# A three-layer compressed interaction network in fp32: PE transposes moved to the end of a period, ReLU copies split in two, four places for high parts

## The reference

```python
LAYER_SIZE = [200, 200, 200]; SPLIT_HALF = True        # x: (512, 39, 32)
for i in range(3):
    z = jnp.einsum('bmd,bnd->bmnd', x, hidden).reshape(B, -1, D)
    cur = jnp.einsum('bcd,co->bod', z, Ws[i]) + bs[i][None, :, None]
    cur = jax.nn.relu(cur)
    if i != 2: hidden, direct = cur[:, :100, :], cur[:, 100:, :]
    else:      direct = cur
    finals.append(direct)
result = jnp.sum(jnp.concatenate(finals, axis=1), axis=-1)   # (512, 400)
```

## Time and profile before

| | |
|---|---|
| median of 3 runs | 3346.16 us (3346.16, 3346.29, 3316.85) |
| profiled execution, own time | 3314.96 us |
| its span, first to last instruction | 3313.2 us |
| PE, DVE, ACT busy | 2899.5, 2725.9, 1619.3 us |
| mean granted TensorE clock | 0.922 of full |

### The profile page before, as it was taken

The page is one execution under the profiler, slowest core; times in us unless marked ns, Lnnn a source line. Parts: engine busy times, 40 slices in busy tenths (PEclk is TensorE's granted clock), DMA queues, the critical chain, the costliest instruction groups (busy, mean ns, idle before and its releaser), DMA issues.

```text
span 3313.2 us, 51577 instructions
## 1 busy us (share of the span) xinstructions
PE 2899.5 (88%) x17960; PEld 2844.1 (86%) x17960; DVE 2725.9 (82%) x2725; ACT 1619.3 (49%) x2212; POOL 0.7 (0%) x7
## 2 busy tenths in 40 slices
PE   3788888888888889998998899989998999899988
PEld 3788888888888888888888888888888888888888
DVE  5788888888888888888888888888887888788877
ACT  3454554555455454445445444444444444544444
POOL 0000000000000000000000000000000000000000
PEclk8899999999999998988889889889898898988988
DMA  8433433333434334333344343333333343334331
GB/s 192 112 102 103 107 90 104 105 90 108 113 103 111 99 91 109 100 90 90 104 117 103 92 109 99 90 91 105 105 91 92 104 106 91 90 95 111 94 90 52
DMA packets 230963, 335.32 MB, mean 101 GB/s; under 512 B 28072, under 2 KB 165268, under 8 KB 230804
## 3 DMA queue, kind: packets, MB, share of 16 engines
q1 hardware_dynamic: 230902, 334.50, 38.7%
HBM read 329.71 MB, written 6.60 MB: 102 GB/s over the span
## 4 chain that ended last, share of the span: by engine, by line
PE 72%; issue 9%; DVE 8%; ACT 8%; DMA 1%; SPq 1%; DVEq 0%; ACTq 0%
PE acc L734 49%; PE acc L735 22%; DVE z_low L411 6%; ACT z_high L588 4%; ACT hid L613 2%; ACT hid L611 1%; DVE z L395 1%; PE turned L743 1%; DVE z L407 1%; DMA xb<-x_by_unit 0%; DVE s L425 0%; DMA xb<-in_L_rec_b_dram 0%; ACT w_split L623 0%; ACT hid L610 0%; DMA z<-w_rows_again 0%
## 5 line engine op out<-in xcount | busy, mean ns | idle before, releaser
L734 PE MATMUL acc<-w_split,z_high 128*128 128x400 f32 (+1 forms) x8832 | 2866.9, 388 | 403.2 <-DVE z_low L411 401.6
L735 PE MATMUL acc<-w_split,z_low 128*128 128x200 f32 (+1 forms) x8832 | 2345.4, 266 | 0.0
L734 PEld LDWEIGHTS acc<-w_split,z_high 128*128 128x128 f32 (+1 forms) x8832 | 1783.3, 202 | 457.8 <-DVE z_low L411 399.7
L735 PEld LDWEIGHTS acc<-w_split,z_low 128*128 128x128 f32 (+1 forms) x8832 | 1811.6, 205 | 0.0
L588 ACT ACTIVATE z_high<-z 128x1024 fp32r<-128x1024 f32 (+2 forms) x1152 | 1179.1, 1024 | 1214.5 <-DVE z L407 488.6
L411 DVE TENSOR_TENSOR z_low<-z,z_high 128x1024 fp32r<-128x1024 f32 (+2 forms) x1152 | 1354.3, 1176 | 507.9 <-ACT z_high L588 507.6
L407 DVE TENSOR_TENSOR z<-hid,xb 128x1024 f32<-128x1024 f32 (+1 forms) x1024 | 1213.9, 1186 | 4.3 <-ACT hid L613 4.3
L610 ACT ACTIVATE hid<-turned 96x1024 f32<-96x1024 f32 (+1 forms) x130 | 131.0, 1008 | 423.2 <-PE turned L743 423.2
L613 ACT ACTIVATE hid<-turned 32x256 f32<-32x256 f32 (+1 forms) x390 | 144.1, 370 | 4.5
L395 DVE TENSOR_TENSOR z<-x_left,x_right 118x896 f32<-118x896 f32 x128 | 138.9, 1085 | 2.1 <-DMA x_right<-x_by_unit 2.1
L432 DVE SCALAR_TENSOR_TENSOR direct<-s,direct 128x400 f32<-128x400 f32 (+2 forms) x133 | 72.8, 547 | 18.4 <-DVE s L425 3.6
(11 more groups left out here) (26 smaller groups left out, 46.9 us busy)
## 6 DMA issues: line engine op xcount, KB each, us to landing
xb<-x_by_unit SPq DMA_DIRECT2D x384, 384.0 KB, 4.4
x_right<-x_by_unit SPq DMA_DIRECT2D x384, 136.5 KB
xb<-x_by_unit SPq DMA_DIRECT2D x384, 128.0 KB, 5.0
xb<-x_by_unit SPq DMA_DIRECT2D x128, 336.0 KB
xb<-x_by_unit SPq DMA_DIRECT2D x128, 84.0 KB
x_left<-x_by_unit SPq DMA_DIRECT2D x384, 19.5 KB
stage<-in_L_rec_W_dram SPq DMA_DIRECT2D x5, 600.0 KB, 9.4
x_by_unit<-stage SPq DMA_DIRECT2D x12, 160.0 KB, 3.2
```

Source lines behind the costliest of these rows:

```text
L734: nc.tensor.matmul(a[:, 0:2 * O], z_high[slot][0:rows, tok], w, start=(c == 0), stop=False, skip_group_check=True)
L735: last = nc.tensor.matmul(a[:, 0:O], z_low[slot][0:rows, tok], w[:, 0:O], start=False, stop=(c == chunks - 1), skip_group_check=True)
```

## The change

PE transposes at the end of a period, behind M8, and no longer behind M0 of the next. ACT's `dup` moves to the end of the period too, behind H8. `hidden` takes one layer at a time: the tile of layer 1 (for layer 2 of the same unit) is written behind H2 and `second_half2`, and that of layer 0 (for layer 1 of the next unit but one) behind H4. `hid` is now kept by layer, with a semaphore for each, in one tile `mixed` that also stages weights and x. `z_high` has four places; Hk waits for Mk-4, and Lk has a wait of its own for Mk-3 (`freed`). Since nine pieces and four places do not fit two periods, a loop pass is now four periods, and the last three periods of every tile are written out. At the start, layer 1 of unit 0 is done piece by piece among the splits of W1, PE waits for each weight piece alone, the pairs of unit 2 are loaded ahead of W2, and two pieces of W2 are split ahead of period 1. The three copies of a turned x tile stand together behind H5 in the period that has them.

```diff
-RING = 3
+RING, HIGH_RING = 3, 4
-HEAD = 5
-def loop_end(r):
-    return D - 1 if r < TILES - 1 else D - 3
+HEAD, LOOP_END, LOOP = 5, D - 3, 4
...
             def lows(number, slot, rows, n):
                 dve.wait_ge(high, number + 1)
+                dve.wait_ge(freed, number + 1)
...
             def highs(number, slot, rows, n):
-                act.wait_ge(freed, number + 1)
+                act.wait_ge(freed, number + 1 - (HIGH_RING - RING))
                 act.wait_ge(product, number + 1)
...
-            def hidden(a, b, step, par):
-                h, t = hid[par][:, a:b, :, :], turned[:, 0, 0:2 * P].rearrange("p (l t) -> p l t", t=P)[:, a:b, :]
+            def hidden(l, u, par, step):
+                h, t = hid[l + 1][:, par, :, :], turned[:, 0, l * P:(l + 1) * P]
                 act.wait_ge(turned_in, step)
...
ACT, period:
                 highs(base, slot(0), P, group_chunks(0))
-                    dup(a1, 2, ended(n - 1))
                 highs(base + 1, slot(1), P, group_chunks(1))
-                    hidden(a1, 2, ended(n - 1), 1 - par)
                 highs(base + 2, slot(2), P, group_chunks(2))
                     second_half2(base - 1)
+                hidden(1, n - 1, 1 - par, ended(n - 1))
                 highs(base + 3, slot(3), P, group_chunks(3))
                     highs(base + 4, slot(4), L0_ROWS, L0_CHUNKS)
+                if not final:
+                    hidden(0, n + 1, 1 - par, ended(n - 1))
                 highs(base + q, slot(q), P, group_chunks(0))
...
                 highs(base + q + 3, slot(q + 3), P, group_chunks(3))
+                if not final:
+                    dup(a, b, ended(n))
...
PE, period:
                 multiply(1, base, slot(0), 0)
-                if not second:
-                    transpose(a1, 2, ended(n - 1))
                 multiply(1, base + 1, slot(1), 1)
...
+                    multiply(2, base + q + g, slot(q + g), g)
+                if not final:
+                    transpose(a, b, ended(n))
...
DVE, start:
             product0(1, 1, 1)
+            at = first(0)
+            product12(1, 0, 0, 0, at, at)
             lows(1, 1, L0_ROWS, L0_CHUNKS)
...
+            product12(1, 0, 0, 1, at + 1, at + 1)
+            lows(at, at, P, group_chunks(0))
             low_piece(3, 1, 2)
```

More of the change, by code:

```diff
@@ L165, in cin_kernel @@
         turned_in = sem("turned_in")
-        hid_in = sem("hid_in")
+        hid_in = {l: sem(f"hid{l}_in") for l in (1, 2)}
         direct_in = sem("direct_in")
@@ L347, in _ @@
                     period(r, d, r * D + d)
[L348 to L351, removed]
+                with sp.Fori(0, (LOOP_END - HEAD) // LOOP) as i:
+                    for j in range(LOOP):
+                        period(r, HEAD + j, i * LOOP + (r * D + HEAD + j))
+                for d in range(LOOP_END, D):
                     period(r, d, r * D + d)
@@ L489, in _ @@
             add(0, 1).then_inc(direct_in, 1)
[L492 to L498, removed]
+            product0(2, at + GROUPS, at + GROUPS)
+            lows(at + 3, at + 3, P, group_chunks(3))
             low_piece(5, 2, 0)
+            low_piece(6, 2, 1)
+            dve.wait_ge(w_low_done, 7)
+            stage_zeros(2)
             def period(r, d, n, base, sl):
@@ L638, in _ @@
             high_piece(1, 1)
-            hidden(0, 1, 1, 0)
+            hidden(0, 0, 0, 1)
             highs(1, 1, L0_ROWS, L0_CHUNKS)
+            at = first(0)
+            highs(at, at, P, group_chunks(0))
             high_piece(1, 2)
@@ L643, in _ @@
             dup(0, 1, 2)
+            highs(at + 1, at + 1, P, group_chunks(1))
             high_piece(1, 3)
-            at = first(0)
-            for g in range(GROUPS):
-                highs(at + g, slot_of(at + g), P, group_chunks(g))
-                if g == 1:
-                    hidden(0, 1, 2, 1)
-            highs(at + GROUPS, slot_of(at + GROUPS), L0_ROWS, L0_CHUNKS)
+            hidden(0, 1, 1, 2)
+            highs(at + 2, at + 2, P, group_chunks(2))
+            highs(at + 3, at + 3, P, group_chunks(3))
+            highs(at + GROUPS, at + GROUPS, L0_ROWS, L0_CHUNKS)
             high_piece(2, 0)
+            high_piece(2, 1)
             def period(r, d, n, base, sl):
@@ L808, in _ @@
                     n = r * D + d
[L809 to L813 removed]
+                    period(r, d, n, first(n), first(n))
+                with pe.Fori(0, (LOOP_END - HEAD) // LOOP) as i:
+                    for j in range(LOOP):
+                        period(r, HEAD + j, i * LOOP + (r * D + HEAD + j), first(i * LOOP + (r * D + HEAD + j)), first(HEAD + j))
+                for d in range(LOOP_END, D):
                     n = r * D + d
[L815 removed]
+                    period(r, d, n, first(n), first(n))
             at = first(UNITS)
```

159 lines of the change are left out of this document (72 added, 87 removed).

## The result

The changed kernel takes 2780.3 us in the median of four runs (2779.56 to 2781.59); the kernel before took 3341.5 in four (3316.85 to 3346.29). The ratio is 0.833, with a 95% interval of 0.829 to 0.838: 17% less. The profiled execution took 2781.59 us, 0.6 us over the forecast of 2781.

A forecast was written before the change was run, and what follows sets the result against it. The loop PE, ACT, DVE, PE with its pause bounds the kernel; without it DVE does, at 21.11 us per period. 3314.96 - 512.0 (steady) - 13 (start) - 8.1 - 0.5 (end) = 2781 us; forecast 2755 to 2815, range 2755 to 2905.

The forecast's parts named there:

- DVE is the next bound, 0.6 us above PE: Steady period without the pause: DVE has 21.11 us of work, PE 20.5, ACT 12.5.
- H5's room: ACT's H5 ends at 14.7 and L5 needs it at 15.1: 0.4 us to spare, the tightest place.
- H3's room: ACT's H3 ends at 9.8 and L3 needs it at 10.8: 1.0 us to spare.
- The fourth place: Fourth place for high parts: raises H0's room against M6 from 1.3 to 3.3 us, buys tolerance and no time.
- the wait that is satisfied anyway: Lk's added wait for Mk-3: taken as 0; bounds 0 and 0.8 us per period or 100 us.
- the loop of four: Loop pass of four periods, 1120 PE instructions instead of 560: jumps back taken as costing 0.
- Rival 1: ACT late at H5 or H3, so DVE waits each period: 2815 to 2905 us; chance 0.24 (ACT or the waits late).
- rival 2: Longer loop body fetched anew at each of 24 jumps, 4.4 us each, 106 us: about 2885 us; chance 0.08.
- rival 4: PE's wait for `dup` at period end replaces the old stall, periods stay 25.25 us: 3302 or unchanged; chance 0.03.
- Rival 3: Three short PE pauses keep the clock low: 3463 us at half the time, chance 0.03; partial 2830 to 3115, chance 0.04.
- the 2 us for periods with extras: Some ten periods with split `directs` and output sends, three with x turned: together 2 us of added cost.
- my walk: Start laid out step by step: Z0 of period 1 at 68.2, its sums at 98.5 us, 13 us gained.

The follow-up runs named there:

- experiment 7: Changed kernel with DVE's `directs` addition cut from 400 columns to 16, so outputs are wrong: 2740.0 us (0.823), period 20.79.
- experiment 10: Changed kernel with `directs` placed behind Z4 instead of ahead of it: 2752.9 us (0.827), period 20.88.
- experiment 8: Changed kernel with `directs` cut to 16 columns and product Z6 cut from 8 chunks to 1 in the loops: 2708.9 us (0.814), period 20.53.
- experiment 6: Changed kernel with four small unused ACT copies, PSUM to PSUM, added ahead of H5: 2820.3 us (0.848), period 21.42.
- experiment 3: Changed kernel with both groups of ReLU copies together behind H2 and `second_half2`, instead of the second behind H4: 2846.4 us (0.853), period 21.62.
- experiment 4: Changed kernel with three places for high parts instead of four: 2781.4 us (0.834), period 21.12.
- experiment 9: Changed kernel with a loop body of eight periods instead of four: 2808.4 us (0.844).
- experiment 2: Changed kernel with both groups of ReLU copies ahead of H2, transposes left at the end of the period: 3001.1 us (0.900), period 22.87.
- experiment 5: Changed kernel with transposes back behind M0 and both groups of ReLU copies ahead of H2: 3451.5 us (1.038), period 26.47.
- experiment 1: Changed kernel with the transposes back behind M0 and the copies left in their new places: 2782.4 us (0.834), period 21.11.
- experiment 12: Kernel before with only its single `hidden` call moved from ahead of H2 to behind H2 and `second_half2`: 2817.4 us (0.844), period 21.31.
- experiment 11: Changed kernel with the `directs` additions moved from DVE to GpSimd, their ReLU done on ACT in place: 2834.5 us (0.852).

## Why the prediction was right

**The bound.** "DVE is the next bound, 0.6 us above PE" held on both counts. The period came out at 21.10 us against 21.11 predicted, and experiments 7 and 10 show that it is DVE's: work or waiting taken from DVE shows in the time. PE's own period is 20.46 us in experiment 8, 0.64 below. The page of the kernel after does not tell this: its chain of work that ended last puts 66% of the span on PE and 18% on DVE, with both engines 97% busy.

**The layout.** No wait comes back. H5's room, called the tightest place at 0.4 us, is 0.39 in the trace, and experiment 6 used it up. H3's room was put at 1.0 us and is 1.28; experiment 3 spends it. The transposes wait once, for 1.1 us. The copies in two groups stand in idle time, with 1.73 us each, the 1.7 of the prediction (1526.98 to 1528.71).

**What was costed at nothing.** The fourth place (experiment 4), the wait that is satisfied anyway (DVE's spacing is that of before), the loads (120 GB/s; DVE waits for one of them, 2.0 us in the whole run, against 2.1 before) and the loop of four cost nothing. For the loop experiment 9 shows where this ends: twice the length pays 28 us.

**The other rivals.** Rival 1 (ACT late), rival 2 (refetching) and rival 4 (the stall replaced) do not show in the changed kernel; the first two appear when the room is spent (experiments 2, 3 and 6) or the body doubled (9). The price of rival 2 was worked out for 24 jumps; six passes in each of four tiles are 20 jumps back, which makes it some 2870 instead of 2885.

**The clock** is granted in full from 200 to 2600 us. Rival 3, in which three short pauses keep it low, is refuted further than was asked: with a pause of 1.20 us in every period (experiment 2) it stays at 1.00, while one of 3.55 (experiment 5) brings it to 0.50 for 6.80 us.

**Terms that were off.** Three, by 2.7, 1.9 and 1.1 us, and that they nearly cancel is luck: all on one side they would have made it 6 us off.
- The steady part gained 514.7 us instead of 512.0: the 2 us for periods with extras were some 0.4 (2616.84 less 124 times 21.10), and the period is 0.01 shorter.
- The start gained 11.1 us instead of 13. The chain that ended last, in order of time, for this stretch of the kernel after (start, us, what):

```profile
54.95 10.42 DMA mixed<-in_L_rec_W_dram
...
65.40 1.54 ACT w_split L618
...
66.97 1.83 DVE w_split L366
...
70.40 1.22 DVE z L398
```

  The second W2 piece lands at 65.4, and I had put it at 63; Z0 follows at 70.40 instead of 68.2. From there to the sums are 30.2 us, where my walk had 30.3. So period 1 itself is shorter by 10.4 us (40.6 to 30.2), nearly as in the walk, and of the 3 us ahead of it the loads left 0.7 (71.09 to 70.40).
- Behind the last sums 0.6 us was lost, where a gain of 0.5 was put. PE stands 3.7 us near the end in both kernels. The clock over those last stretches was 0.93 before and 0.87 after:

```profile
2753.20:2779.80 26.60, 19.42 (x113) 18.93 (x111) 13.91 (x17) 7.74 (x14) 0.00 (x0) 0.87 0.02 7
```

**What the prediction did not say** is which move the gain hangs on. It treats the transposes, `dup` and `hidden` as one step, and argues mostly from the transposes' end at 4.7 us with 4 us to spare. The runs show that this spare time is hardly used: the place of the copies decides, and with it the transposes could have stayed (at no cost in experiment 1, with the joint copies at 0.2 us per period in experiment 12). "ACT writes hid in two groups" was costed right, at nothing, but its worth, 66 us against one group of the same ten copies, was not worked out. It is a gain only because the copies by layer are ten instructions of 3.46 us instead of five of 2.60: without copies H3 would have 3.01 us of room (1.28 and 1.73), by which five joint ones would fit.

**What stays open**: the gain at the start was read from the traces, and not run by itself. How the part of a jump's cost beyond DVE's own stop divides in experiment 9 is not told apart.

## What to carry to other kernels

On an engine that works through its queue in order, put a small job behind the operation that the bound engine waits for next, as late as its own reader allows, and ask of each such place how much idle time it has; the producer of that job matters only where its reader would otherwise start earlier. Two moves that open the same loop are not two gains: run them one by one, in the old kernel too, and fill the square. When one engine is the bound, look at its starts, not its durations: a dependent operation right behind a short one costs more than two that don't depend on each other.

## What the runs showed of the hardware

- A DVE operation of 400 columns starts 0.5 us behind the 200-column one whose result it reads, and an independent one 0.27 us behind it (experiment 10, 27 us in all).
- GpSimd's 128x400 addition took 10.7 us beside a DVE that runs without a gap, and DVE's own operations stayed within 3 ns in the mean. The 128x200 one took 10.3 us beside a busy DVE and 0.61 beside an idle one (experiment 11).
- Four small ACT copies from PSUM to PSUM took 0.64 us, 0.16 each, where the same shape from PSUM to SBUF steps by 0.28 (experiment 6).
- Loop bodies of 560 and 1120 PE instructions jump back for nothing; with one of 2240 each jump costs 3.5 us, of which DVE stands 2.85 by itself (experiment 9).
- Pauses of 1.20 and 0.49 us in a period left TensorE's clock at 1.00 (2.4 GHz); one of 3.55 us had 0.50 (1.2 GHz) for 6.80 us around and behind it (experiments 2 and 5).
